# A recurrence of 512 dependent steps: scores also with keys on partitions, input products fetched from DRAM, and the work between the steps in another order

## What is computed

```
def step(h, x_t):                       # h: 4 x 128
    score = einsum('bsh,bh->bs', enc_hiddens, h @ W)      # 4 x 77
    attn = softmax(score)
    context = einsum('bs,bsh->bh', attn, enc_hiddens)     # 4 x 128
    gx = concatenate([x_t, context]) @ kernel + bias      # 4 x 384
    gh = h @ recurrent_kernel                             # 4 x 384
    z = sigmoid(xz + hz); r = sigmoid(xr + hr)
    cand = tanh(xh + r * hh)
    h_new = z * h + (1 - z) * cand
```

## Time and profile before

| | |
|---|---|
| median of three runs | 3068.23 us |
| the profiled execution, its own time | 3084.98 us |
| its span, first to last instruction | 3082.8 us |
| the 512 steps, first to last new state | 1002.9 to 2961.5 us |
| granted TensorE clock, mean | 0.97 |
| busy: PE, DVE, ACT, POOL | 88%, 70%, 56%, 32% |

### The profile page before, as it was taken

The page is one execution under the profiler, slowest core; times in us unless marked ns, Lnnn a source line. Parts: engine busy times, 40 slices in busy tenths (PEclk is TensorE's granted clock), DMA queues, the critical chain, the costliest instruction groups (busy, mean ns, idle before and its releaser), DMA issues. The chain is left out here.

```text
span 3082.8 us, 131006 instructions
## 1 busy us (share of the span) xinstructions
PE 2726.5 (88%) x54163; PEld 1797.8 (58%) x54163; DVE 2146.9 (70%) x8143; ACT 1713.6 (56%) x5762; POOL 997.4 (32%) x1992
## 2 busy tenths in 40 slices
PE   7999999888778999899999899999989888888769
PEld 4666666575455555565566566666656545444439
DVE  5666666773432888788888688888878766777653
ACT  4666666533443666576776576666657544333322
POOL 2000000231110566355766355555535311000015
PEclk9999999999878999999999999999999999999989
DMA  4000000000011000000001010000001000000013
GB/s 142 5 5 7 5 6 5 11 1 1 19 30 42 7 14 31 4 31 17 11 10 31 4 44 4 11 7 11 28 3 33 8 4 3 4 3 4 3 45 80
DMA packets 41077, 56.47 MB, mean 18 GB/s; under 512 B 6238, under 2 KB 27688, under 8 KB 40360
## 3 DMA queue, kind: packets, MB, share of 16 engines
q1 hardware_dynamic: 36392, 42.46, 4.4%
q0 software_dynamic: 4096, 5.67, 1.0%
HBM read 42.45 MB, written 5.67 MB: 16 GB/s over the span
## 5 line engine op out<-in xcount | busy, mean ns | idle before, releaser
L2183 POOL TENSOR_TENSOR gru_terms<-gru_states,gru_signs 128x8 f32<-128x8 f32 x512 | 104.2, 204 | 1147.5 <-DVE gru_states L2470 1043.5
L2103 ACT ACTIVATE gru_p<-gru_ps_sg,gru_negmax 128x78 f32<-128x78 f32 x512 | 167.6, 327 | 331.1 <-DVE gru_negmax L2439 326.3
L2107 ACT ACTIVATE gru_th_r<-gru_pre_r 128x32 f32<-128x32 f32 x512 | 119.4, 233 | 406.6 <-DVE gru_pre_r L2450 406.6
L1691 PE MATMUL gru_ps_sg<-ctx_gate_w,gru_p_t 128*4 128x64 f32 x12288 | 267.3, 220 | 0.1
L368 ACT ACTIVATE self_probs<-self_sc,self_negmax 128x512 f32<-128x512 f32 x256 | 174.4, 685 | 166.1 <-DVE self_negmax L425 166.1
L2159 POOL TENSOR_SCALAR bg_probs<-bg_probs,bg_arsum 128x256 f32<-128x256 f32 (+2 forms) x192 | 241.0, 1255 | 19.0
L1936 PE MATMUL gru_ps_sg<-score_w,gru_states 128*4 128x78 f32 x4096 | 165.1, 234 | 74.2 <-DVE gru_states L2470 73.0
L2439 DVE TENSOR_REDUCE gru_negmax<-gru_ps_sg 128x1 f32<-128x78 f32 x512 | 121.8, 238 | 146.9 <-PE gru_ps_sg L1936 142.3
L2443 DVE STREAM_TRANSPOSE gru_p_t<-gru_p 128x96 f32<-128x96 f32 x512 | 142.7, 279 | 112.7 <-ACT gru_p L2103 112.5
L1940 PE MATMUL gru_ps_own<-late,gru_states 128*4 128x128 f32 x4096 | 208.4, 276 | 0.0
L1691 PEld LDWEIGHTS gru_ps_sg<-ctx_gate_w,gru_p_t 128*4 128x4 f32 x12288 | 172.2, 86 | 38.3 <-issue 0.3
(11 more groups left out here) (421 smaller groups left out, 7302.4 us busy)
## 6 DMA issues: line engine op xcount, KB each, us to landing
bg_w<-in_moe_w SPq DMA_DIRECT2D x48, 256.0 KB, 3.0
bg_wa<-in_wqkv SPq DMA_DIRECT2D x24, 192.0 KB, 2.3
moe_w<-in_moe_w SPq DMA_DIRECT2D x16, 256.0 KB, 2.9
best_w_sb<-in_ec_w SPq DMA_DIRECT2D x16, 256.0 KB
cross_scratch<-ctab_raw SPq DMA_DIRECT2D x16, 154.0 KB
cross_outs<-cross_scratch POOLq DMA_DIRECT2D x4, 576.0 KB, 6.3
late<-in_late SPq DMA_DIRECT2D x1, 2269.5 KB
self_w_sb<-in_wqkv SPq DMA_DIRECT2D x8, 192.0 KB, 2.3
```

What stands on the lines that cost most here:

```text
L1691: last = pe.matmul(bank[32 * c:32 * c + B, 0:hi - lo], p_t[:, 32 * k:32 * k + B], gate_w[:, k, 96 * c + lo:96 * c + hi], start=k == 0, sto ...
L2103: act.activation(p[:, 0:CTX + 1], ps_s[:, 0:CTX + 1], ACT.Exp, bias=negmax[:, 0:1], accum_out=total[:, 0:1])\
```

## The change

Scores are made twice. Once as before in shape (batches on partitions, now with each batch's state broadcast to 32 columns so that all 32 rows of a tile hold the same scores), only for the maximum. And once with keys on partitions: 12 small products with `score_w` as weights (32 columns each) and the 4 state columns moving, into `ps_t`, 128x12. ACT takes the exponential of these, into `p_t`, which the gate products read directly. There is no accumulator read, no transpose of the weights and no spreading matmul: `gate_w` has two more columns per chunk which hold ones for real keys, so the r products (now 34 columns, without the candidate's) also yield the sum, and DVE takes its reciprocal from `ps_r` before `pre_r`. The candidate's and z's products are one group of 64 columns, and one DVE operation handles both.

The products of x_t are no longer made per step, apart from the first 8 steps of each 128. For each group and batch, one product of 120 rows x 384 columns (`x_rows_of`) is copied by ACT, stored to a DRAM tensor by SP, and read back in chunks of 8 steps (`load_rows`); DVE adds them when it takes `ps_own`.

Background pieces stand elsewhere: on PE nearly all behind the gate products (`after_gates`), with a few between own and gate products (`ahead_of_gates`); the down product is whole; `hidden` on DVE is in two halves, before and after the maximum; ACT's and POOL's pieces are regrouped. Fill matmuls go from 8 to 2 in a step with nothing else. SP issues its loads in the order of t.

```
-            dve.scalar_tensor_tensor(out=gate_w[:, k, :], ...)
+            dve.scalar_tensor_tensor(out=by_chunk[:, :, 0:32], ...)
+            dve.scalar_tensor_tensor(out=by_chunk[:, :, GATE_C:GATE_ALL], ...)      # GATE_C, GATE_ALL = 34, 98
+            dve.tensor_copy(by_chunk[:, :, 32:GATE_C], is_key ...broadcast_to([P, 4, 2]))
...
+        STAGES = {2: {"project": 0, "squares": 0, "take_v": 1, "sums": 1, "rows": 2, "turn": 2, "take_qk": 2, "scores": 3,
+                      "max0": 4, "exp0": 4, "scale0": 4, "max1": 5, "exp1": 5, "scale1": 5, "probs0": 5, "turned0": 5, "probs1": 6, "turned1": 6,
+                      "values": 6, "take_out": 7, "out": 7, "add": 8},
...
+            def load_rows(k):
+                sp.wait_ge(s_xout, 16 * B * (k * CHUNK // P + 1))
+                sp.wait_ge(s_own, (k - 1) * CHUNK)
+                for b in range(B):
+                    sp.dma_start(x_in[b:P:32, k % 2, :, :], x_products[k * CHUNK:(k + 1) * CHUNK, b, :].rearrange("t (c g) -> c t g", c=4))
...
+            def ahead_of_gates(t):
+                for g, n, m in units_at(t, "turn"):          # PACE 3
+                for g, n, m in units_at(t, "out"):           # PACE 3
+                for g, n, m in units_at(t, "probs1"):        # PACE 2
+                        turn_probs(g, n, m, 1)
...
             for t in range(S):
-                wait_positive(pe, s_xt, t // P)
-                for c in range(4):
-                    pe.matmul(ps_own[32 * c:32 * c + B, 0:96], x_t[:, B * t:B * (t + 1)], x_w[:, c, :], start=True, stop=False, ...)
-                busy = t and before_scores(t - 1)
-                wait_positive(pe, s_u, t)
-                pe.matmul(ps_s[:, 0:CTX + 1], mask_l, mask_r[:, 0:CTX + 1], start=True, stop=False, ...)
+                busy = t and after_gates(t - 1)
+                wait_positive(pe, s_own, t)
+                if not from_rows(t): ...                      # t % 128 < 8: x products as before
+                wait_positive(pe, s_precz, t)
+                pe.matmul(ps_t, mask_l, mask_r, start=True, stop=False, skip_group_check=True)
                 if not busy:
-                    for i in range(6):
-                        fill_in(2 * P, ps_tz)
+                    for i in range(2):
+                        fill_in(2 * P, ps_sr)
                 pe.wait_ge(s_h, t + 1)
                 for b in range(B):
+                    last = pe.matmul(ps_s[32 * b:32 * b + 32, :], state(t)[:, b:b + 1].broadcast_to([P, 32]), score_w[:, b, 0:CTX + 1], ...)
                 last.then_inc(s_score, 1)
+                for k in range(3):
+                    for b in range(B):
+                        last = pe.matmul(ps_t[32 * b:32 * b + 32, B * k:B * k + B], score_w[:, b, 32 * k:32 * k + 32], state(t), ...)
+                last.then_inc(s_turnedmm, 1)
                 ...                                           # own products
-                after_own(t)
+                ahead_of_gates(t)
                 pe.wait_ge(s_exp, t + 1)
-                for c in range(4):
-                    last = pe.matmul(ps_t[32 * c:32 * c + B, 0:2], spread, total[:], ...)
-                fill_in(P, ps_own)
-                pe.wait_ge(s_pt, t + 1)
-                gate_products(ps_g, 0, 64).then_inc(s_rcmm, 1)
-                pe.wait_ge(s_rt, t + 1)
-                gate_products(ps_z, 64, 96).then_inc(s_zmm, 1)
+                gate_products(ps_r, 0, GATE_C).then_inc(s_rmm, 1)
+                gate_products(ps_cz, GATE_C, GATE_ALL).then_inc(s_czmm, 1)
...
-                act.activation(p[:, 0:CTX + 1], ps_s[:, 0:CTX + 1], ACT.Exp, bias=negmax[:, 0:1], accum_out=total[:, 0:1])
+                act.wait_ge(s_turnedmm, t + 1)
+                act.activation(p_t[:], ps_t, ACT.Exp, bias=negmax[:, 0:1]).then_inc(s_exp, 1)
...
+                for g, n, m in units_at(t, "sums"):           # POOL, now ahead of scale_probs
+                    qk_norms(g, n, m)
...
-                dve.tensor_copy(own[:, 0:256:2], ps_own[:, 0:P]).then_inc(s_own, 1)
-                dve.wait_ge(s_exp, t + 1)
-                dve.transpose(p_t[:], p[:]).then_inc(s_pt, 1)
-                dve.wait_ge(s_total, t + 1)
-                dve.reciprocal(rtotal[:], ps_t[:, 0:1]).then_inc(s_rt, 1)
-                before_gates(t)
+                after_maximum(t)
+                    dve.tensor_tensor(own[:, 0:256:2], ps_own, x_in[:, k % 2, t % CHUNK, :], ALU.add).then_inc(s_own, 1)
+                dve.wait_ge(s_rmm, t + 1)
+                dve.reciprocal(rtotal[:], ps_total).then_inc(s_rt, 1)
                 dve.scalar_tensor_tensor(out=pre_r[:], ...)
-                dve.scalar_tensor_tensor(out=own[:, 193:256:2], ...)
-                dve.scalar_tensor_tensor(out=pre_z[:], ...)
+                dve.wait_ge(s_czmm, t + 1)
+                dve.scalar_tensor_tensor(out=c_and_z, in0=ps_cz, scalar=rtotal[:, 0:1], in1=own[:, 64:192:2], ...)
```

442 lines of the change are left out of this document (248 added, 194 removed).

## The result

The changed kernel takes 3033.39 us (median of four runs, 3027.16 to 3035.75) against 3071.49 for the kernel before in the same session: a ratio of 0.9868, 95% interval 0.9849 to 0.9887. It is faster by 1.3%. The forecast was 2905 with a range to 2985, so the direction was right and the size wrong: 128 us too much.

What follows compares the result with a forecast made beforehand. The recurrence's 512 dependent steps, 64% of the span, bound the kernel. Savings of 186 us, less 6, 12 and 4, net 164: profiled execution 3085 to 2921, median forecast 2905, range 2,845 to 2,985.

Steps and rivals of the forecast that it cites:

- quiet step: Recurrence step with no background pieces between; forecast to go from 3.69 to 3.28 us, 192 of them at most.
- the clock's case: Fewer fills let PE's clock fall to 1.2 GHz in quiet steps: 0.7 us each, 2,970 to 3,040; chance 0.11.
- the forecast's own signs of being wrong: Exponential released by turned products instead of the maximum, quiet steps above 3.5, or DVE's own addition waiting on a DMA.
- The chain: Dependent operations of one step, scores to new state: `pre_r` at +1.61 against +2.03, exponential 0.21, turned products inside the maximum.
- the rule that the prediction cites: Weight loads overlap a running matmul only where row groups differ; by it the turned products would stand on the path.
- The slower rival: Turned products' loads queue and delay the exponential: 0.40 on each of 512 steps, 205 us, around 3,110; chance 0.06.
- Attention: Attention steps: 3.45 (g = 1), 3.75 (g = 2, PE waiting for POOL's scaled row in even steps), 3.38 (g = 3).
- Experts: 96 expert steps bound by PE's own loop: 3.61 us from 3.92, saving 30 us.
- The sum: Savings over all recurrence steps, together 186 us, net 164 after costs of large products, stalls and set-up.
- the stalls of the large products: In 16 steps large x products and copies cost 6 us; 12 copies waiting for the last store about 12.

Runs made afterwards that it cites:

- the two experiments on the fills: Changed kernel with six fill matmuls instead of two per step without pieces: 2946.07 us; kernel before with six cut to two and two single fills removed: 3143.27 us.

## Why the prediction was wrong

**The clock, the step that failed.** The forecast priced every quiet step at 2.4 GHz and gave the clock's case a chance of 0.11. That case came true. Its price per step was 0.7, scaled up from one step of the old chain that was 0.61 longer; over whole steps it is 0.61 (3.91 less 3.30). In the changed kernel's profile the recurrence took 1913.6 us, with six fills 1830.2; 83 us at 0.61 are some 136 steps at the low level, not all 192. The mean clock of the recurrence says the same (columns as above):

```profile
1004.50:2918.10 1913.60, 1662.46 (x50165) 1076.32 (x50163) 1329.26 (x5589) 1032.71 (x3982) 849.11 (x1847) 0.85 0.06 17
```

With two levels, 1.00 and 0.50, a mean of 0.85 is some 570 us at the low one; with six fills the mean is 0.99, some 40 us. The difference is again some 136 steps of 3.91.

That the case was named at 3,040 for all 192 steps, and 3033 was measured, is partly luck: the clock cost 87 us and not 134, and some 40 us of optimism elsewhere (below) made up the difference. What I held against the clock's case was that the gate products grow no shorter and that scores, turned and own products add up to more. The trace after shows that this does not carry: PE's records fill 78% of the stretch at 1.2 GHz and 66% of the one at 2.4. The busy share on the page could not tell the level here; it was higher at the low clock, where the same instructions last longer. Two of the forecast's own signs of being wrong came: quiet steps above 3.5, and the exponential released by the turned products, in 129 of the 512 steps. The Trainium skill, "TensorE: Matmul & The Clock Gate", section "What's actually happening", has the throttled state as the one that holds unless activity lifts it. I had cited it and set it aside for an argument from busy time; here the two experiments on the fills agree with it.

**The chain.** Right, but for the size of the exponential. 3.28 a quiet step, measured 3.30; `pre_r` 1.61 behind the scores' start, measured 1.67. The exponential took 0.27, not 0.21, within its bounds. The turned products ended at +0.51, inside the maximum's time. The loads of four tiles with the same rows run over each other and over matmuls (24 pairs in 0.35), as the earlier trace rows had suggested for two tiles. That is against the rule that the prediction cites from the Trainium skill, "TensorE: Matmul & The Clock Gate", section "The mechanism". The slower rival is ruled out for the change as it is. Doubling the products shows how small the margin is: 0.26 more of them made the step 0.20 longer, so some 0.06 us were free at 2.4 GHz, and at 1.2 GHz none are.

**Attention.** In the stretches shown above g = 1 takes 3.47 for 3.45, g = 3 3.41 for 3.38, g = 2 3.79 for 3.75. For g = 2 that is the later part. Its earlier one, where PE also makes x products of single steps and the large ones of the group, is much longer:

```profile
L2551 DVE TENSOR_TENSOR_SCAN gru_states<-gru_factors,gru_terms x27: 181/183/321, 1420.6 to 1528.4; 128x12 f32<-128x12 f32 x27
```

That is 4.15 a step. Over all its steps g = 2 takes some 3.92, against 4.01 before, and so gained some 6 us where 16 were forecast. In the later part the size is right and the reason wrong. The even step of the changed kernel, answering to the earlier trace rows:

```profile
1554.68 1.26 POOL L2243 TENSOR_SCALAR bg_probs<-bg_probs,bg_arsum 128x384 f32<-128x384 f32 x1
...
1555.57 0.42 PE L2021 MATMUL gru_ps_ox<-late,gru_states 128*4 128x128 f32 x8
...
1555.99 0.55 PE L1830 MATMUL gru_bg_turn<-early,bg_probs 128*128 128x128 f32 x3
...
1557.50 1.25 POOL L2243 TENSOR_SCALAR bg_probs<-bg_probs,bg_arsum 128x384 f32<-128x384 f32 x1
...
1557.66 0.56 DVE L2540 TENSOR_TENSOR_SCAN gru_c_in<-gru_th_r,gru_own 128x64 f32<-128x64 f32 x1
```

The scaled row is ready at 1555.94, PE's own products end at 1555.99, and the transposes start then: there is next to no wait. The gates are late because PE comes late out of the step before and has the transposes to do.

**Experts.** 3.61 was forecast, PE-bound; it is PE-bound, at 3.71 in most steps, every fourth 3.87, single ones 5.05. An expert step of the changed kernel, PE only, from its scores to the next:

```profile
1373.54 0.34 PE L2010 MATMUL gru_ps_sr<-score_w,gru_states 128*32 128x78 f32 x8
...
1374.55 0.37 PE L1755 MATMUL gru_ps_sr<-ctx_gate_w,gru_p_t 128*4 128x34 f32 x24 [0.25 <-ACT gru_p_t L2188]
...
1377.24 0.27 PE L2010 MATMUL gru_ps_sr<-score_w,gru_states 128*32 128x78 f32 x4
```

Of the 0.10 in most steps 0.07 stand ahead of the gates, which come at +1.01 in place of +0.94; nearly all of that is the exponential (0.27 for 0.21). The rest of the loop was summed at 2.67 and takes 2.70. In every fourth step DVE's addition to `y` and half of `hidden` stand ahead of the maximum and make it 0.16 more. The steps of 5.05 are held scans.

**The sum with the clock given back.** Recurrence 1958.6 before, 1830.2 with six fills: 128 us where 164 were forecast. By stretches of the two traces, attention of g = 1 brought 20 where I had 25, g = 2 6 for 16, g = 3 27 for 36, experts some 10 for 30, the other steps 65 for 79. These 128 us already contain the stalls of the large products, for which I had taken off 18. About 40 us of optimism in all, which would have stayed inside the range; the 87 us of the clock did not.

## What to carry to other kernels

Matmuls whose product nobody reads can be what pays for the clock: when a change shortens or empties PE's work in a stretch, ask first which instructions kept the clock up there, and test that with more fills before looking at anything else. Read a stretch's mean from its first step to its last: the steady part of attention of g = 2 hid steps of 4.15. And look where a DVE scan with two operands in SBUF falls beside POOL's long product of two operands: beginning 0.06 ahead of it the scan took 0.29 us, beginning 0.25 behind it 1.16.

## What the hardware showed unexpectedly

**POOL holds DVE's scans.** All `c_in` scans and all state scans by line (columns: shapes, count, busy us, mean ns, idle before), of the kernel before, the changed one, and the one with half of the down product ahead of the gates:

```profile
L2459 DVE TENSOR_TENSOR_SCAN gru_c_in<-gru_th_r,gru_own 128x64 f32<-128x64 f32 x512 | 150.0, 293 | 2.5 <-ACT gru_th_r L2107 2.5
L2470 DVE TENSOR_TENSOR_SCAN gru_states<-gru_factors,gru_terms 128x12 f32<-128x12 f32 x512 | 93.4, 182 | 30.3 <-ACT gru_factors L2113 1.7 <-DVE gru_terms L2466 0.8
```

```profile
L2540 DVE TENSOR_TENSOR_SCAN gru_c_in<-gru_th_r,gru_own 128x64 f32<-128x64 f32 x512 | 170.3, 333 | 57.9 <-ACT gru_th_r L2191 4.6
L2551 DVE TENSOR_TENSOR_SCAN gru_states<-gru_factors,gru_terms 128x12 f32<-128x12 f32 x512 | 126.5, 247 | 20.0 <-DVE gru_terms L2547 2.1 <-ACT gru_factors L2197 0.7
```

```profile
L2542 DVE TENSOR_TENSOR_SCAN gru_c_in<-gru_th_r,gru_own 128x64 f32<-128x64 f32 x512 | 238.1, 465 | 58.9 <-ACT gru_th_r L2193 5.6
```

The kernel before loses next to nothing; the change brings 20 us of held `c_in` scans and 33 of held state scans, the latter nearly all in expert steps, where PE is late anyway; in the third the held `c_in` scans are 88 us. A scan that begins behind the start of POOL's product of 512 columns lasts until that product is over (state scans 546 to 556 ns [above], ending 0.04 behind it; `c_in` 0.15 behind it). Beside its scaling of 384 columns the scan is held for 0.27 only, and beside its powers on 4 columns not at all. State scans that begin 0.7 us into a scaling of 512 columns aren't held either (attention of g = 3, 181 to 183 ns above). The Trainium skill, "SBUF — State Buffer", section "Who interferes with whom", says that a DVE instruction with two SBUF inputs contends with a GpSimd instruction that reads SBUF, and that the one that comes second is blocked until the first is over. For the product the traces agree, with 1.16 for 0.29; for the scaling the hold was shorter than that instruction (0.56 in all, with 0.5 of the scaling still to go), and for the powers there was none.

**More fills than were needed bought nothing.** With two fills the 300 us from 2600 on were all at 1.2 GHz (0.50); with four, 140 us of such steps stood at 1.00. The step from two to four gave all of the 85 us, the one from four to six nothing that the runs can tell (2948.74 and 2946.07). With two fills the clock also stood at 1.00 for a while, in the 26 us at 2429. PE made x products up to 2444.9 there; from 2462 to 2500, where it made none, the clock was at 0.51. Whether they kept it up was not tested with two fills in the changed kernel.
